# A chain of model stages on one core: which loads and norms the routed experts and the feed-forwards wait for

## The reference

```python
x = x + _L0_ffn_ref(_layernorm(x), ...)      # routed experts
    scores = sigmoid(x @ router_w.T); sfc = scores + e_bias
    # 4 of 8 groups by their two best, then 8 of 64 experts, weights normalised, times 2.5
    h = silu(x @ Wg) * (x @ Wu) * coef;  out = h @ Wd + shared expert
...
for l in range(4):                           # inner model
    h = h + attention(_ln(h, ln1_w[l], ln1_b[l]))
    fn = _ln(h, ln2_w[l], ln2_b[l])
    h = h + gelu(fn @ W1[l].T + b1[l]) @ W2[l].T + b2[l]
...
x = _layernorm(x + performer(x), ln1_g, ln1_b)
x = _layernorm(x + gelu(x @ w1 + b1) @ w2 + b2, ln2_g, ln2_b)
```

## Time and profile before

| | us |
|---|---|
| median of three runs | 6509.09 (6506.85 to 6525.96) |
| profiled execution | 6521.95, around a span of 6520.1 |
| PE, DVE, ACT, POOL busy | 88%, 65%, 43%, 28% of the span |
| DVE stands before the routed experts' first instruction | 24.20 |
| ACT stands before `f_xnT` at the four feed-forwards | 58.0 in all |
| ACT stands before `g_xnT` behind the performer | 13.91 |

### The profile page before, as it was taken

The page is one execution under the profiler, slowest core; times in us unless marked ns, Lnnn a source line. Parts: engine busy times, 40 slices in busy tenths (PEclk is TensorE's granted clock), DMA queues, the critical chain, the costliest instruction groups (busy, mean ns, idle before and its releaser), DMA issues. The chain is left out here.

```text
span 6520.1 us, 121590 instructions
## 1 busy us (share of the span) xinstructions
PE 5750.7 (88%) x38509; PEld 3558.5 (55%) x38509; DVE 4215.9 (65%) x9620; ACT 2834.4 (43%) x4602; POOL 1843.6 (28%) x2616
## 2 busy tenths in 40 slices
PE   8996999999996999879987998889988989875677
PEld 5773444444443676457754776457754556533464
DVE  6874666666665776367744776367745756577764
ACT  4553222222222555435543555445544645433344
POOL 5440000000002554155523554155520012151012
PEclk9998999999998999989998999889999999887798
DMA  4332333333334554055512553055510000000002
GB/s 133 104 104 86 97 97 97 98 95 96 96 99 108 141 147 119 7 139 148 148 41 78 147 147 104 11 143 147 147 34 4 0 3 0 4 4 0 0 2 59
DMA packets 526321, 526.95 MB, mean 81 GB/s; under 512 B 55699, under 2 KB 436706, under 8 KB 503781
## 3 DMA queue, kind: packets, MB, share of 16 engines
q1 hardware_dynamic: 526004, 523.15, 29.0%
HBM read 337.88 MB, written 185.07 MB: 80 GB/s over the span
## 5 line engine op out<-in xcount | busy, mean ns | idle before, releaser
L362 DVE TENSOR_REDUCE a_mx<-a_unit 128x2 f32<-128x512 f32 (+1 forms) x1920 | 1296.2, 685 | 584.5 <-PE a_unit L538 571.6
L452 ACT ACTIVATE a_prob<-a_slot 128x1536 f32<-128x1536 f32 x640 | 929.2, 1452 | 749.0 <-PE a_slot L561 454.3
L536 PE MATMUL a_unit<-a_sk,a_sq 96*128 96x256 bf16 (+3 forms) x5120 | 753.8, 250 | 77.1 <-DMA a_sk<-a_kscratch 55.2
L1127 ACT ACTIVATE f_silu<-f_pG 128x512 f32<-128x512 f32 x528 | 315.0, 598 | 934.7 <-PE f_pG L1200 920.6
L538 PE MATMUL a_unit<-a_maskq,identb 128*128 128x256 bf16 (+1 forms) x1920 | 604.0, 315 | 0.0
L1069 DVE TENSOR_TENSOR f_gated<-f_spread,f_silu 128x512 f32<-128x512 f32 x512 | 354.6, 693 | 348.7 <-ACT f_silu L1127 308.4
L1179 PE MATMUL f_pO<-f_hidden,f_wd 128*128 128x512 f32 x1056 | 545.9, 599 | 13.5 <-DVE f_hidden L1071 13.3
L536 PEld LDWEIGHTS a_unit<-a_sk,a_sq 96*128 96x128 bf16 (+1 forms) x5120 | 383.9, 99 | 313.1 <-issue 124.5
L1200 PE MATMUL f_pG<-f_xnT,f_wg 128*128 128x512 f32 x1056 | 542.3, 595 | 0.0
L1204 PE MATMUL f_pU<-f_xnT,f_wu 128*128 128x512 f32 x1056 | 540.1, 593 | 0.0
L554 PE MATMUL a_slot<-a_sq,a_sk 98*128 98x256 bf16 (+1 forms) x2560 | 427.5, 275 | 109.0 <-DMA a_sq<-a_mscratch 102.1
(11 more groups left out here) (397 smaller groups left out, 11253.3 us busy)
## 6 DMA issues: line engine op xcount, KB each, us to landing
f_spread<-f_scratch SPq DMA_DIRECT2D x1024, 128.0 KB, 2.9
a_sq<-a_qscratch SPq DMA_DIRECT2D x128, 768.0 KB, 5.7
a_sk<-a_kscratch SPq DMA_DIRECT2D x160, 384.0 KB, 6.6
a_qscratch<-a_parts SPq DMA_DIRECT2D x288, 192.0 KB, 2.2
a_qscratch<-a_parts SPq DMA_DIRECT2D x288, 128.0 KB, 2.2
a_kscratch<-a_parts SPq DMA_DIRECT2D x160, 192.0 KB, 2.2
a_kscratch<-a_parts SPq DMA_DIRECT2D x160, 128.0 KB, 2.1
a_qscratch<-a_parts SPq DMA_DIRECT2D x288, 64.0 KB, 1.8
```

What stands on the lines that cost most here:

```text
L362: v.tensor_reduce(dst, src, op=ALU.max, axis=AX.X, negate=True).then_inc(red_done, 1)
L452: act.activation(prob[gr % 2][:, :], slot[:, :], ACT.Exp, scale=SCALE).then_inc(exp_done, 1)
L536: pe.matmul(bank[:, at * wide:(at + 1) * wide], q, sk[b][0:KM, gr * GH + h, 0:wide], start=(at == 0), stop=False)
L1127: act.activation(silu[c % 2][:, :], pG[c % 2][:, :], ACT.Silu).then_inc(silu_done, 1)
```

## The change

**Routed experts.** The three router loads are issued first and have a semaphore of their own, `router_in`. DVE and PE wait for it alone at their start; PE waits for the six weight loads (`w_in`) right before the first `pG`. ACT waits for neither and begins with a one-column sigmoid.

**Feed-forward in the layer loop.** A new class `FeedHead` holds the weights, the buffers of the first norm, and four semaphores outside the layer loop. The attention before it issues the five loads behind its own. In its step 31 DVE makes the statistics of block 0; in step 32, behind the last store, it applies the norm to block 0 and makes the statistics of block 1; POOL makes both reciprocal roots. The feed-forward leaves steps -3 and -2 out on DVE and POOL (`begun` is -1). ACT begins with a one-column Gelu.

**Feed-forward behind the performer.** Here only the loads move, into the performer (`begun` is -3: no step is left out). `gain` is still loaded in the feed-forward, with a semaphore that POOL waits for in step 1.

```diff
@@ attention @@
+                if head is not None:
+                    head.load(sp, head_w, layer)
...
+                    if head is not None and isinstance(n, int) and n >= SEQS - 1:
+                        blk = n - SEQS + 1
+                        g.wait_ge(head.stats_done, blk + 1)
+                        ln_rstd(g, chain, head.moments, head.veps, head.mhalf, head.rstd, eps, head.rstd_done, apart)
...
+                    if head is not None and once(n, SEQS - 1):
+                        v.drain()
+                        ln_stats(v, chain, rows(store, 0, BT), head.stats, head.moments, head.stats_done)
+                    if head is not None and once(n, SEQS):
+                        v.wait_ge(head.rstd_done, 1)
+                        ln_apply(v, rows(store, 0, BT), head.moments, head.rstd, head.xn).then_inc(head.xn_done, 1)
+                        v.drain()
+                        ln_stats(v, chain, rows(store, BT, BT), head.stats, head.moments, head.stats_done)
@@ new class @@
+class FeedHead:
+    W_IN = 16 * 5
+    def load(self, sp, w, layer=None):
+        for dst, name in ((self.lnw[:, :], "ln"), (self.w1[:, :], "w1"), (self.b1[:, :], "b1"), (self.w2[:, :, :], "w2"),
+                          (self.b2[:, :], "b2")):
+            sp.dma_start(dst, w[name] if layer is None else w[name][layer]).then_inc(self.w_in, 16)
@@ feed_forward @@
-                g.memset(mhalf[:, :], -0.5).then_inc(setup, 1)
-                g.wait_ge(setup, 1)
-                g.wait_ge(w_in, W_IN)
                 def step(n, b):
+                    if isinstance(n, int) and n < head.begun:
+                        return
+                    if gb is not None and once(n, 1):
+                        g.wait_ge(gain_in, 16)
...
             @block.scalar
-                act.wait_ge(w_in, W_IN)
+                act.activation(warm[:, :], core["ident"][:, 0:1], ACT.Gelu)
+                act.wait_ge(w_in, head.W_IN)
@@ routed_experts @@
+                for dst, src in ((wr[:, :], w["router"]), (bias[:, 0, :], w["bias"].partition_broadcast(P)),
+                                 (tri[:, :], core["tri"].partition_broadcast(P))):
+                    sp.dma_start(dst, src).then_inc(router_in, 16)
                 for dst, src in ((wg[:, 0:CH * P], w["wg"]), (wg[:, CH * P:], w["swg"]), (wu[:, 0:CH * P], w["wu"]),
-                                 (wu[:, CH * P:], w["swu"]), (wd[:, 0:CH, :], w["wd"]), (wd[:, CH, :], w["swd"]),
-                                 (wr[:, :], w["router"]), (bias[:, 0, :], w["bias"].partition_broadcast(P)),
-                                 (tri[:, :], core["tri"].partition_broadcast(P))):
+                                 (wu[:, CH * P:], w["swu"]), (wd[:, 0:CH, :], w["wd"]), (wd[:, CH, :], w["swd"])):
                     sp.dma_start(dst, src).then_inc(w_in, 16)
...
             @block.vector
-                v.wait_ge(w_in, W_IN)
+                v.wait_ge(router_in, ROUTER_IN)
...
             @block.scalar
-                act.wait_ge(w_in, W_IN)
+                act.activation(oT[:, 0:1], core["ident"][:, 0:1], ACT.Sigmoid)
...
             @block.tensor
-                pe.wait_ge(w_in, W_IN)
+                pe.wait_ge(router_in, ROUTER_IN)
...
                     if now:
+                        if once(n, 0):
+                            pe.wait_ge(w_in, W_IN)
                         pe.wait_ge(xnT_done, n + 1)
@@ performer, stage_a1, stage_l2 @@
+                head.load(sp, head_w)
...
+        head = FeedHead(nc, stack, "f1h_", -1)
...
+        head = FeedHead(nc, stack, "g2h_", -3)
```

More of the change, by code:

```diff
@@ L156, with attention @@
 KPART = [0, 1, 2, 0, 1, 0]
-def attention(nc, core, tag, store, eps, w, kept, layer=None, arriving=None):
+def attention(nc, core, tag, store, eps, w, kept, layer=None, arriving=None, head=None, head_w=None):
     rel = kept.rel
@@ L295, in _ @@
                 chain = Chain(g)
+                if head is not None:
+                    g.memset(head.mhalf[:, :], -0.5)
                 chain.link(g.memset(mhalf[:, :], -0.5))
@@ L687, in feed_forward @@
         k = Held(nc, stack, tag)
[L688 to L692, removed]
+        w1, w2, lnw, b1, b2 = head.w1, head.w2, head.lnw, head.b1, head.b2
+        stats, moments, veps, rstd, mhalf, xn = head.stats, head.moments, head.veps, head.rstd, head.mhalf, head.xn
+        w_in, stats_done, rstd_done, xn_done = head.w_in, head.stats_done, head.rstd_done, head.xn_done
+        warm = k.sb("warm", [P, 1])
+        xnT = [k.sb(f"xnT{b}", [P, BLK]) for b in range(2)]
         act_out = k.sb("act_out", [P, CH, BLK]); oT = k.sb("oT", [P, BLK])
@@ L699, in feed_forward, with _ @@
         pO = [k.ps(f"pO{b}", [P, BLK]) for b in range(2)]; pR = k.ps("pR", [P, BLK])
-        (w_in, setup, apart, stats_done, rstd_done, xn_done, t_pe, xnT_done, h_pe, gelu_done, o_pe, o_done,
+        (gain_in, apart, t_pe, xnT_done, h_pe, gelu_done, o_pe, o_done,
          r_pe, r_taken, stats2_done, rstd2_done, affine_done, x_done) = k.sem(
-            "w_in setup apart stats_done rstd_done xn_done t_pe xnT_done h_pe gelu_done "
+            "gain_in apart t_pe xnT_done h_pe gelu_done "
             "o_pe o_done r_pe r_taken stats2_done rstd2_done affine_done x_done")
-        W_IN = 16 * (5 if gb is None else 6)
         with nc.Block() as block:
[L707 to L713, removed]
+            if gb is not None:
+                @block.sync
+                def _(sp):
+                    sp.dma_start(gain[:, :, :], gb.partition_broadcast(P)).then_inc(gain_in, 16)
             @block.gpsimd
@@ L834, in _ @@
                 deep(pe, step)
+        for s in head.held.sems:
+            nc.gpsimd.sem_clear(s)
         k.clear()
@@ L1467, in top2_experts, with performer @@
         k.clear()
-def performer(nc, core, tag, w):
+def performer(nc, core, tag, w, head, head_w):
     M = 32
@@ L2579, in _ @@
                 kept.fill(g)
+        head = FeedHead(nc, stack, "f1h_", -1)
         with nc.Fori(0, 4) as layer:
-            attention(nc, core, "a1_", core["h"], 1e-6, part_of(a, "a1_"), kept, layer)
-            feed_forward(nc, core, "f1_", core["h"], 1e-6, part_of(a, "f1_"), True, layer)
+            attention(nc, core, "a1_", core["h"], 1e-6, part_of(a, "a1_"), kept, layer, None, head, part_of(a, "f1_"))
+            feed_forward(nc, core, "f1_", core["h"], 1e-6, part_of(a, "f1_"), True, head)
         kept.held.clear()
@@ L2590, in stage_l2 @@
 def stage_l2(nc, core, a):
-    performer(nc, core, "p2_", part_of(a, "p2_"))
-    feed_forward(nc, core, "g2_", core["h"], 1e-6, part_of(a, "g2_"), False, None, a["n2_gb"])
+    with ExitStack() as stack:
+        head = FeedHead(nc, stack, "g2h_", -3)
+        performer(nc, core, "p2_", part_of(a, "p2_"), head, part_of(a, "g2_"))
+        feed_forward(nc, core, "g2_", core["h"], 1e-6, part_of(a, "g2_"), False, head, a["n2_gb"])
 def stage_q2(nc, core, a):
```

19 lines of the change are left out of this document (14 added, 5 removed).

## The result

| | before | after |
|---|---|---|
| median of 6 runs each, us | 6510.53 | 6479.34 |
| lowest run, us | 6506.85 | 6466.15 |
| ratio of the runs, 95% interval | | 0.9943 (0.9926 to 0.9959) |
| profiled execution, span in us | 6520.1 | 6482.4 |
| granted TensorE clock, mean | 0.945 | 0.946 |

The change gains 31 us between the medians; the ratio says 37, with 27 to 48 as its interval. One of the six runs of the changed kernel took 19935.74 us, three times as long as all others; the ratio leaves it out, the median of six holds it, and without it the median is 6478.33.

The account below looks back on a forecast made before the run. TensorE was busy for 88% of the span, so only seams between stages could gain: 16.2 (experts) + 13.4 (four layer-loop feed-forwards) + 4.3 (behind the performer) = 33.9 us, from 6509.1 to 6475 us; range 6460 to 6496.

Parts of the forecast that it names:

- Routed experts: Start of the routed experts: router loads issued first, `tri` landing after 2.4 us, whole chain 16.2 us earlier; bounds 15.1, 18.6.
- The big loads: Routed experts: last of six weight loads lands at about 568.2, product wanted at 573.1, wait covered with 4.9 us to spare.
- Head: Layer-loop feed-forward, VectorE's first instruction to first product before, new head after: 9.87 us becomes 2.33, saving 7.54 (fourth layer 7.44).
- tail: End of the layer loop's attention: norm of block 0, statistics and root of block 1 add 4.13 us, uncovered.
- handover: Between attention and feed-forward: barrier, about fifty semaphore clears, barrier; stays 4.30 us from store to first instruction.
- The net of 3.4 per layer: Layer-loop seams: 7.54 saved minus 4.13 added gives 3.4 us, 3.3 in the fourth layer; 13.4 us over four layers.
- Table loads: Early sigmoid in the experts credited nothing (bounds 0, 1.3); feed-forward's Gelu load and warm-up, 1.50 us, finish after the transposes.
- Performer: Feed-forward behind the performer: GpSimd starts at 5672.12 instead of 5676.44, 4.3 us gained; bounds 4.1 to 4.4.
- Clock: TensorE starts at the lower clock as before: neither gain nor loss counted, 1 us allowed for each of five seams.
- nothing was fetched late at the heads: Rival: instruction fetches of about 3.4 us at four feed-forward starts cancel the net gain there, giving 6489; chance 9%.
- The router loads were faster: Rival at the routed experts: big loads take the DMA engines first, `tri` lands at 568 as before, giving 6491; chance 7%.
- no jump costs more: Rival: attention loops fetch anew at each jump, 4 jumps in 4 layers at 3.45 us, 55 us, giving 6530; chance 4%.

Follow-up runs that it names:

- e7: Changed kernel with the sync queue waiting for the three router loads before issuing the six big ones; ratio 0.9936 (0.9922 to 0.995) to the kernel before.
- e6: Changed kernel with VectorE waiting for the router loads at the bias and TensorE at the logits; ratio 0.9943 (0.9927 to 0.996) to the kernel before.
- e10: Changed kernel with statistics, root and norm taken out of the layer loop's attention, leaving loads and memset; ratio 0.9940 (0.9927 to 0.9954) to the kernel before.
- e5: Changed kernel without ScalarE's two early one-column activations (Gelu, Sigmoid); ratio 0.9927 (0.9912 to 0.9942) to the kernel before.

## Why the prediction was right

The time, 6475, and its sum, 33.9, stand beside 6479 and the 33.2 us read at the seams. That the sum came within 0.7 us is partly luck: the routed experts were put 1.8 us too high and the seams of the layer loop 1.1 too low. Step by step:

- **Routed experts, 16.2 forecast, 14.4 measured.** The mechanism is as told; the term mis-sized is the landing of `tri`. I took 2.4 us from a 32 KB load that I called one on an idle queue; the one of its three loads whose landing the profile has stood third of four, with 64 KB issued behind it. `tri` took 4.4, beyond the 3.5 of my bound, so the floor of 15.1 was too high. e7 prices most of it: 1.5 of the 2.0 us come from the 2 MB loads behind it. The other 0.5 stays open; `tri` is spread over all partitions by a broadcast, the row's load is not.
- **The big loads.** Forecast to land at 568.2 with 4.9 us of slack; they landed at 569.6, with 4.7. The slack was right only because two misses matched: counted from the first issue, `swd` landed at 21.4 us and not 19.5, as it took 16.7 us and not 14.7, and the chain came 1.8 us later too. e6 shows that the slack was real: with VectorE 5.2 us earlier the product waits for `swd`.
- **Head, 2.33 forecast, 2.22 measured; tail 4.13 and 4.04; handover 4.30 and 4.25.** All three within 0.12, each from a row of the same work elsewhere; the head's path was another one than forecast (see the table loads). The net of 3.4 per layer was 3.6. The last three layers clear their semaphores in 3.3 us instead of 3.6, which is the difference between 10.5 and 10.16.
- **What the prediction did not see.** It subtracted head and tail from one another and was right in the difference, but did not ask what the loads alone would give. e10 answers: all of it. The sum of the parts was correct and its reading, that the norm made early saves something, was not.
- **Table loads.** Credited nothing in the experts, rightly (e5). In the feed-forward I let ScalarE's pair be late last, 0.3 us behind the transposes. It was TensorE: its transposes began 0.19 us behind ScalarE's first instruction, and the copy started 0.12 us behind their end, before the change 0.10. Without the pair the seam is as long (e5), so 2.33 came near 2.22 by luck. The Trainium skill (ScalarE: Activation LUTs, "What ACT_TABLE_LOAD costs") puts 2.66 us on a switch of tables, load and drain together; as an estimate from this figure the copy would have started no sooner than 2610.43 + 2.66 = 2613.09. The trace disagrees: it ran at 2611.83, the warm-up 1.29 us behind the start of the load.
- **Performer, 4.3 and 4.3.**
- **Clock.** Nothing counted, and in the layer loop nothing to be seen: TensorE's four transposes at the new seams take 1.09 us, as they did before, and the higher level comes 3.4 to 5.5 us behind the first product before, 4.0 to 5.2 after. Behind the performer it came 5.6 us behind the first product before and 3.2 after; the rest of that stage is 1.3 us shorter, a little more than the 1 us that I allowed.
- **Rivals.** ScalarE's first instruction ran at the release and TensorE's 0.2 us behind it, so nothing was fetched late at the heads. The router loads were faster. The attentions took 583.2 us before and 583.7 after in the mean, and the routed experts from the first product to the end of their stage 1426.6 and 1427.2: no jump costs more. The 3.45 us that priced two of the rivals has ScalarE's silu as what came last, so how much of it was a fetch is not shown.

## What to carry to other kernels

Work moved ahead of a barrier pays only as far as something there covers it: read the gaps of that engine and put it in front of the last thing the barrier waits for, not behind it. Before the norm is moved, count what the waits alone give; here that was everything. And where a seam recurs, look at what it consists of: one instruction per semaphore was a third of what was left of it, and taking them out of all stages gave some 25 us where the whole change had given 37.

## What the runs showed of the hardware

- A clear of one semaphore by GpSimd takes 0.07 us in a row of them (503 in the profile, 33.8 us in all); one clear over a run of some fifty neighbouring numbers took 0.31 us.
- A 32 KB load that stood third in the queue landed after 4.3 to 5.6 us in the kernels with 2 MB loads issued behind it at once, and after 2.9 with none (e7). The first of the three, 1.4 us ahead of the big ones, took 1.6 to 1.9 us either way. So being issued ahead of large loads does not shield a small one that they follow within half a us. The Trainium skill (DMA: Bandwidth & Descriptors, "Queues, rings and completion order") says that later data may be written before earlier data in one queue; no run here shows that, as the nine loads landed in the order of their issue in every profile.
- Over the 52 attentions of the layer loop in 13 profiles, the length goes from 577 to 599 us with the time that TensorE spends at the lower of its two clocks, 1.2 GHz, within it: 45 to 77 us, 0.7 us longer for each such us, correlation 0.91. Two profiles of one kernel can differ by 10 us and more in this way, which is why 4 us had to be read at the seam. What moves the clock from run to run is open.
